# Where the folded weights, keys and values of the first cross attention are made in a twelve-stage decoder kernel

## What is computed

```python
x = x + _L0_attn_ref(_layernorm(x), ...)      # causal, 16 heads of 8
x = x + _L0_xattn_ref(_layernorm(x), ctx_768, mask, g_norm, null_kv, Wq, Wkv, Wout, g_out)

def _L0_xattn_ref(x, context, mask, g_norm, null_kv, Wq, Wkv, Wout, g_out):
    x = layer_norm(x, g_norm)
    q = x @ Wq                                # 16 heads of 64
    k, v = split(context @ Wkv)               # 77 keys and values
    k, v = concat(null_k, k), concat(null_v, v)   # 78 of each
    sim = where(full_mask, (q * s) @ (k * s).T, lowest)
    out = softmax(sim) @ v
    return layer_norm(out @ Wout, g_out)
```

## Time and profile before

| | us |
|---|---|
| median of three timed runs | 1457.36 |
| lowest and highest of them | 1456.46, 1460.57 |
| the profiled execution | 1448.4 |
| span of its instructions | 1446.6 |
| TensorE busy | 1344.5 (93% of the span) |
| VectorE busy | 932.2 (64%) |
| ScalarE busy | 672.6 (46%) |
| chain of waits, share of TensorE | 73% |
| mean granted TensorE clock | 0.978 |

### The profile page before, as it was taken

One profiled execution on the slowest core, in us unless ns is written; L12 is line 12 of the kernel. 1 busy time (PEld: TensorE's weight loads), 2 busy tenths in 40 slices (PEclk: granted clock), 3 DMA queues, 4 the chain that ended last, 5 costly groups with the idle time before them and its releaser, 6 DMA issues.

```text
span 1446.6 us, 29623 instructions
## 1 busy us (share of the span) xinstructions
PE 1344.5 (93%) x11718; PEld 872.5 (60%) x11718; DVE 932.2 (64%) x1890; ACT 672.6 (46%) x1697; POOL 344.6 (24%) x373
## 2 busy tenths in 40 slices
PE   8999899999999989999889978899999999999986
PEld 6767556445666676667787667764435556654434
DVE  5775655535576646356665376678888886677755
ACT  4887443333677645344401255425557777740002
POOL 4000231001011110004204011157777556300001
PEclk9999999999999999999999999999999999999998
DMA  3000102310000000000033002101020011599980
GB/s 133 3 2 2 33 6 102 119 46 29 2 2 3 2 18 0 10 12 5 2 143 114 19 12 87 31 15 45 30 58 16 17 27 20 126 215 251 252 205 15
DMA packets 25353, 80.61 MB, mean 56 GB/s; under 512 B 5243, under 2 KB 7306, under 8 KB 24834
## 3 DMA queue, kind: packets, MB, share of 16 engines
q1 hardware_dynamic: 24354, 75.60, 19.1%
q10 hardware_dynamic: 864, 3.15, 0.8%
HBM read 72.17 MB, written 1.08 MB: 51 GB/s over the span
## 4 chain that ended last, share of the span: by engine, by line
PE 73%; DVE 11%; ACT 7%; DMA 4%; issue 3%; POOL 1%; SPq 0%; DVEq 0%; ACTq 0%; POOLq 0%
PE psum L196 7%; PE psum L2915 6%; PE psum L428 5%; PE psum L2936 5%; PE psum L2629 4%; PE psum L1236 4%; PE psum L2585 4%; PE psum L1230 3%; PE psum L448 3%; PE psum L2599 2%; PE psum L495 2%; PE psum L668 2%; PE psum L2638 2%; DMA heads<-scratch_out_gates 2%; DMA context_v<-scratch_out_gates 2%
## 5 line engine op out<-in xcount | busy, mean ns | idle before, releaser
L196 PE MATMUL psum<-ident 128*128 128x128 f32 x1324 | 167.4, 285 | 9.8 <-DMA ident<-in_ident 4.1
L196 PEld LDWEIGHTS psum<-ident 128*128 128x128 f32 x1324 | 159.6, 199 | 17.7 <-issue 6.5
L187 POOL TENSOR_TENSOR rstd<-var,minus_half 128x4 f32<-128x4 f32 x30 | 31.1, 1037 | 556.7 <-DVE var L144 525.5
L572 DVE TENSOR_REDUCE quad_max<-psum 128x1 f32<-128x128 f32 (+3 forms) x256 | 113.1, 484 | 56.8 <-PE psum L432 54.4
L529 ACT ACTIVATE pt<-psum,quad_max 128x128 f32<-128x128 f32 (+3 forms) x256 | 133.4, 530 | 25.9 <-DVE quad_max L572 25.7
L2936 PE MATMUL psum<-pt,slots 128*128 128x512 f32 x256 | 114.6, 599 | 4.7 <-DVE pt L3090 3.7
L2915 PE MATMUL psum<-slots,xn_t 128*128 128x512 f32 x256 | 113.9, 605 | 3.1 <-DVEq L3061 3.1
L2674 ACT ACTIVATE p<-psum,duo_max 128x512 f32<-128x512 f32 x128 | 86.9, 684 | 42.6 <-DVE duo_max L2709 41.6
L3005 ACT ACTIVATE pt<-psum,p 128x64 f32<-128x64 f32 x256 | 58.0, 393 | 72.6 <-POOL wide L3147 42.0
L2936 PEld LDWEIGHTS psum<-pt,slots 128*128 128x128 f32 x256 | 47.1, 189 | 71.3 <-issue 48.5
L2915 PEld LDWEIGHTS psum<-slots,xn_t 128*128 128x128 f32 x256 | 49.6, 194 | 66.0 <-issue 57.6
(11 more groups left out here) (514 smaller groups left out, 2808.2 us busy)
## 6 DMA issues: line engine op xcount, KB each, us to landing
pt<-scratch_out_gates SPq DMA_DIRECT2D x32, 256.0 KB, 13.2
heads<-scratch_out_gates SPq DMA_DIRECT2D x24, 256.0 KB, 15.6
slots<-in_s_l0f SPq DMA_DIRECT2D x8, 514.0 KB, 3.4
wide<-scratch_gates SPq DMA_DIRECT2D x8, 512.0 KB, 8.0
slots<-in_s_l3v SPq DMA_DIRECT2D x8, 512.0 KB, 3.5
context_v<-scratch_out_gates SPq DMA_DIRECT2D x16, 256.0 KB, 18.1
slots<-in_s_l3o ACTq DMA_DIRECT2D x6, 512.0 KB, 10.3
weights<-in_w_l1a SPq DMA_DIRECT2D x1, 2624.0 KB, 9.3
```

Source lines behind the costliest of these rows:

```text
L196: nc.tensor.matmul(m.ps[bank][:, 0:P], m.ident[:, :], m.ident[:, :], start=True, stop=True, skip_group_check=True)
L572: nc.vector.tensor_reduce(m.quad_max[:, n % 2, g:g + 1], m.ps[g][:, 0:keys], AX.X, ALU.max, negate=True).then_inc(m.quad_negmax, 1)
```

## The change

- `fold_weights` and `project_keys` move into the first three sets of the first attention, in place of its fillers: folded weights in set 0 (banks 4 to 7), six key products in set 1 and two in set 2 (banks 6 and 7). Their copies on ScalarE follow the exponentials: four behind set 0, two in the middle of set 1, one in the middle of set 2.
- The mask row is made by `add_bias`, before set 16 of the attention.
- In the norm, ScalarE copies two folded keys, a half of `x`, two folded keys, the other half of `x`, and the last two folded keys. The last folded keys use banks 4 and 5 instead of 2 and 4.
- The folded values of the first context, four of eight, are made in the norm in place of the fillers, two ahead of the turned tokens and two behind them, in banks 2 to 5. ScalarE copies them behind `xn_t`. The other four are made in units 0 and 1. SyncE waits for all of them, and so do unit 0's on TensorE for the copies of the first four.

The core of the diff:

```diff
@@ l0_attn_tensor
             for j in range(2):
                 copied(m, pe, f"l0v{j}")
-        keep_busy(nc, m, RAMP[i], O_BANK)
+            fold_weights(nc, pe, m)
+        elif i == 1:
+            project_keys(nc, pe, m, (0, 1))
+        else:
+            project_keys(nc, pe, m, (2,))
+            pe.wait_ge(m.ahead_taken, H // 4 + len(KEY_PAIRS))
@@ quad_scalar
                                      accum_out=sum_column(HEAD_OF[g], b, j, qt)).then_inc(m.quad_exp, 1)
+                if beside and (i, g) in beside:
+                    beside[i, g]()
@@ l0_attn_scalar
+    quad_scalar(nc, act, m, a, lambda g, b, j, qt: m.quad_sum[:, b, qt, 4 * g + j:4 * g + j + 1], take_output, None,
+                beside={(0, GROUP - 1): take_weights, (1, 1): lambda: take_keys((0, 1)), (2, 1): lambda: take_keys((2,))})
@@ l0_attn_vector, add_bias
+        dve.wait_ge(m.context_in, 16 * 4)
+        m.dve.done(nc.vector.tensor_scalar(m.mask_low[0:1, :], m.mask_u8[0:1, 0:2 * B * SC], -1.0, BIG, ALU.add, ALU.mult))
...
@@
-FOLD_BANKS = ((4, 5), (0, 1), (2, 4))
+FOLD_BANKS = ((4, 5), (0, 1), (4, 5))
+WEIGHT_BANKS, KEY_BANKS, VALUE_BANKS = (4, 5, 6, 7), (6, 7, 7), (2, 3, 4, 5)
@@ l0_cross_tensor
     fold_keys(nc, pe, m)
-    busy_through_norm(nc, pe, m, 2, 0, 0)
+    for n in range(2):
+        fold_values(nc, pe, m, n, m.ps[VALUE_BANKS[n]]).then_inc(m.ahead_made, 1)
     turn_tensor(nc, pe, m, "l0xn")
-    turned(nc, m, pe, "l0xn")
     pe.wait_ge(m.ahead_taken, FOLDS)
+    for n in range(2, 4):
+        fold_values(nc, pe, m, n, m.ps[VALUE_BANKS[n]]).then_inc(m.ahead_made, 1)
+    for j in range(2):
+        copied(m, pe, f"l0xn{j}")
     pe.wait_ge(m.low_row_ready, 1)
...
-        for n in range(2 * k, min(2 * k + 2, B * H // 4)):
...
+        if k == 0:
+            pe.wait_ge(m.ahead_taken, FOLDS + 4)
+        for n in range(2 * k, min(2 * k + 2, 4)):
+            fold_values(nc, pe, m, 4 + n, fill(m, pe, f"l0xb{n}")).then_inc(filled(m, f"l0xb{n}"), 1)
@@ l0_cross_sync
-    for n in range(B * H // 4 - 2, B * H // 4):
+    sp.wait_ge(m.ahead_taken, FOLDS + 4)
+    for n in range(2, 4):
         copied(m, sp, f"l0xb{n}")
@@ l0_cross_scalar
+    take_keys([(0, 0), (0, 1)])
+    take_x(nc, act, m, "l0y", 2, halves=(0,))
+    take_keys([(1, 0), (1, 1)])
+    take_x(nc, act, m, "l0y", 2, halves=(1,))
+    take_keys([(2, 0), (2, 1)])
     turn_scalar(nc, act, m, "l0xn", scale=w["g_norm"])
+    for n, bank in enumerate(VALUE_BANKS):
+        act.wait_ge(m.ahead_made, FOLDS + n + 1)
+        nc.scalar.activation(values_of(n), m.ps[bank][0:nk, :].rearrange("p (h d) -> p h d", d=P), ACT.Copy).then_inc(
+            m.ahead_taken, 1)
```

## The result

The changed kernel takes 1440.04 us, median of four runs (1438.42 to 1443.89), beside 1456.91 for the kernel before (1453.01 to 1460.57, the three runs of the table above and one more). The ratio is 0.9888, with a 95% interval of 0.9854 to 0.9922. That is 16.9 us less where 12.0 were forecast, and 0.04 us inside the lower edge of the range (1440 to 1452). The profiled execution took 1443.89 with a span of 1442.1, beside 1448.4 and 1446.6 of before. So the two profiled executions are only 4.5 apart. That gap is taken apart further down: the edited stretch gives more than the forecast, and the unedited rest of the program took 10.1 longer in this one execution.

The account below looks back on a forecast made before the run. Bounds: TensorE's chain after the first attention, SyncE's late value copies, and lower-clock stretches. Terms -3.9 - 0.3 - 8.9 + 0.3 + 0.8 = -12.0 gave a 1445.4 us median (profiled 1436.4), range 1440 to 1452.

Parts of the forecast that it names:

- The value copies, -8.9: Cross attention: SyncE's copies start 7.65 us earlier, so unit 8's reduction comes at 178.1 instead of 186.97, -8.9 us.
- Rival (a): Before the cross attention's first values: copies stay last, landing 2 us later, and the clock falls; 1448.7 us, chance 0.12.
- The norm, -0.3: Norm before the cross attention: tokens 1.2 us earlier, less 0.83 for products replacing fillers, rounded to -0.3 us.
- Rival (d): Before unit 0's folds: ScalarE's four early value copies are waited for, none of their 2.1 us hidden; 1447.5, chance 0.03.
- The mask row, +0.8: Set 16 of the first attention: two mask instructions now ahead of the maxima cost their full price, +0.8 us.
- The end of the attention, -3.9: End of first attention to output projection: folded weights and keys leave TensorE there, -3.9 us, bounds -4.9 and -2.9.
- the one that let the fall stay: End of the attention: 3.4 us at the lower clock remain, so the last values take about 2.0 us instead of 1.01.
- the step on the output projection: Before the output projection: x enters the banks after VectorE's copy, 1.9 us earlier than before; GpSimd's scaled output is ready already.
- The prediction's sign: Trace marks if right: first output projection begins at about 143 us, SyncE's value copies near 160.2.
- The first three sets, +0.3: First three sets of the first attention: moved weights, keys and their ScalarE copies replace fillers, +0.3 us, bounds +2.2 and -1.6.
- rival (c): Neither clock fall comes, after 28 or after 134 us: 1.6 and 1.0 us less, 1442.8, chance 0.08.
- Rivals (b) and (e): First sets without fillers: clock at half once more, 1448.8, chance 0.08; or half clock through many sets, 1463.4, chance 0.03.

Follow-up runs that it names:

- values_back: Changed kernel, but all eight folded values made in units 0 to 3 again and fillers back in the norm; 1450.03 us, ratio 0.9954.
- tokens_back: Changed kernel, but ScalarE copies both halves of x behind all six folded-key copies again; 1444.66 us, ratio 0.9928.
- after: The changed kernel itself against the kernel before, first measurement and profiled execution; median 1440.04 us, ratio 0.9888.
- after_again: The changed kernel run once more with no edit, against the kernel before; 1444.59 us, ratio 0.9921.
- copies_late: Changed kernel, but SyncE waits for unit 4's exponentials before its twelve value copies; 1453.35 us, ratio 0.9988.
- best: Changed kernel with the mask row back behind the norm and the attention's last output scaling on VectorE instead of GpSimd; 1438.84 us, ratio 0.9897.

## Why the prediction was right, and where it was off

**The value copies, -8.9.** Measured -8.88, and each step of it held: SyncE begins 7.63 earlier relative to the first scores (7.65 forecast), copies and transposes meet within 0.34 (0.35), and from the first values to unit 8 it takes 2.45 (2.55) instead of 3.83, since the clock no longer falls. The held-back copies show that without the early start nothing of it is left; 1.78 of it also needs the shorter steps. Rival (a), copies last by 2 us, did not come.

**The norm, -0.3.** Measured -0.34, from the two sizes it was made of. The tokens' order alone takes it from 10.00 to 8.92 (values_back), 1.08, and the two value products ahead of the scores then cost 0.74. Taken in the other way round, the products cost 0.92 (10.92 in tokens_back) and the order is worth 1.26. Rival (d) did not come: ScalarE's value copies are not waited for.

**The mask row, +0.8.** Measured +0.73, and given back by the one experiment that moves it.

**The end of the attention, -3.9.** Measured -5.20, beyond its bounds of -4.9 and -2.9; -4.01 in the third execution of the changed kernel, which had the fall of the clock. Two steps of the forecast failed. The first is the one that let the fall stay and hit the last values at 2.0 instead of 1.01. Where the fall came, it did just that (1.94 in tokens_back); but of the seven executions with the moved work and nothing else edited at this place, four had none (after, after_again, values_back, copies_late). The second is the step on the output projection: I put x's way into the banks behind VectorE's copy and took GpSimd for done by then. In fact x goes in 0.20 before that copy starts, in every execution with the moved work, and GpSimd is last: copy 0.69, scaling 1.26 and the handovers make 2.09 from the copy's start to the projection, where my step made 2.46. Taking GpSimd away (best) gave 0.62 more. The prediction's sign, an output projection near 143 and SyncE's copies near 160.2, missed for the same reasons: they stand at 140.27 and 157.68.

**The first three sets, +0.3.** Measured -1.03. The sizes held (folded weights 1.99, between 1.6 and 2.95; a wait of 0.58 for the third key copy), and the moved work costs 0.5 against fillers without a fall. The sign is wrong because the fall of the clock that all three profiled executions of the kernel before have did not come; where it came (after_again), the stretch took 57.53, 0.07 more than before. So what came at both places in this execution is rival (c), to which the prediction gave 0.08. Its 2.6 and the miss of 2.56 (-14.56 less -12.0) agree better than their parts do: the two falls are worth 1.1 and 1.2 here (56.44 against 57.53, 7.20 against 8.39), and the rest is small misses of size. In the other two executions of the changed kernel only one of the two falls was gone. Rivals (b) and (e), more of the lower clock in the first sets, did not come in any of nine executions. The Trainium skill, "TensorE: Matmul & The Clock Gate", section "What's actually happening", says that the chip's look at activity does not start anew with a kernel, so the point at which the clock changes moves from run to run. That may be why a fall is there in one execution and not in the next; no run here tests it. What the three executions of the same instructions do show is that a forecast should carry such a fall as a probability, not as a row that is there.

**The step from the sum to the median.** The sum was made on one profiled execution and moved to the median. At the anchor the three executions of the changed kernel are 14.56, 15.15 and 13.61 ahead of those of before, 1.0% of the kernel, and both timed ratios, 0.9888 and 0.9921, hold 0.990 in their intervals. The two medians are 16.9 and 12.6 below those of the kernel before that were timed with them. So it was luck on which side of the forecast the first median fell and that it stayed inside the range by 0.04; the gain itself is not. Behind the anchor, where nothing is edited, the profiled executions took 1225.0, 1230.7 and 1225.6 us for the kernel before and 1223.4 to 1235.1 for the ten others. Up to the block of 104 fillers the lower clock goes with nearly all of that; the rule of 0.4 us for each us of it, on which some of the expectations rest, is a little low there (0.47). Behind the block the rate of the last stage's loads explains one pair. From the anchor to the block TensorE was at the lower clock for 30.7, 44.5 and 30.7 us in the kernel before and for 41.0 to 54.7 in the others. Whether the earlier arrival causes that or it is chance was not settled.

## What to carry to other kernels

A row of transfers issued one after another is a single item on the path as long as its issue (9.67 us here): the question is when its last input is ready, and moving half of that input's work forward gave 8.9 us, while the shorter steps that came with it gave nothing by themselves. Work that fills an engine's idle time can replace fillers at nearly no cost (0.5 us here for 4.6 us of products), but a small instruction put on the engine that is late costs its whole length (0.73), though it is free one stage later. Cut two traces at marks in the edited stretch before comparing their spans: here the spans differed by 4.5 and by 22.5 for an edit worth 14.6. Where unedited stages differ, cut those too: one block of fillers as a mark told the clock's part from the loads' part.

## What the runs showed of the hardware that I had not expected

- Two executions of the same kernel moved 250 and 287 GB/s in the last stage (window 1300 to 1360), with the DMA engines busy all the time in both, and were 6.8 us apart in the 500 us that hold these loads. The other eleven executions lay at 250 to 261. What sets the rate is open.
- Where TensorE's clock falls differs between executions of the same instructions. One fall cost 1.1 us (with the moved work) to 1.5 (with the fillers) in the first sets, and 1.0 to 1.4 at the end of the attention.
- In 730 us of unedited stages, thirteen executions took 727.8 to 738.6 us, and 0.47 us more for each us in which TensorE was granted 1.2 GHz (30.7 to 54.7 us of it).
